# A mixture-of-experts loop made flat: first weights copied by ScalarE, second weights fetched by SyncE, remainders of up to 40 rows in slots

## The chip, the cores and the metric

The kernel runs on one core of a Trainium2 chip. The metric is the device time of one execution in microseconds (us); a kernel's time is the median of its runs. TensorE is called PE in the profile (PEld is its loading of weights), VectorE is DVE, ScalarE is ACT, GpSimd is POOL, and SyncE, which here only issues transfers, is SP.

## What is computed

The input x has 4 sequences of 512 tokens of 128 numbers, 2048 tokens in all. A windowed and latent attention with gates is followed by a residual sum and a layer norm; then comes a mixture of experts, again with residual sum and layer norm. Only the second part is touched by the change, apart from where a few instructions stand:

```python
h = jnp.mod(x_flat[:, :TOP_K].sum(axis=1).astype(jnp.int32), E)
sel = jnp.stack([h, jnp.mod(h + 1, E)], axis=1)
def step(acc, params):
    e, W1e, b1e, W2e, b2e = params
    w = jnp.any(sel == e, axis=1).astype(x.dtype) / TOP_K
    y = jnp.maximum(x_flat @ W1e + b1e, 0.0) @ W2e + b2e
    return (acc + w[:, None] * y, None)
```

W1 is 8 x 128 x 512, W2 is 8 x 512 x 128, all float32. So each token belongs to one of eight groups by a hash of its normed values, and is computed by expert h and expert h + 1 (modulo 8).

## The kernel before

The attention runs over T = 16 tiles of P = 128 tokens, in a software pipeline of T + 3 steps, written out by hand as one instruction list for each engine. Its last step is L1338 with t = T + 2. As tiles are normed, their hash is taken and GpSimd scatters their rows to a memory area seg, in which every group has a segment of its own (L507 to L515). A row there is 129 numbers: the token and its index.

A group is then worked off in tiles of 128 rows. Every tile needs the two halves of the work, for expert e and for e + 1: columns (turn the rows, L1294), up (four matmuls with W1, L1305, into PSUM banks), relu, down (four matmuls with W2, L1323, L1452 and L1459, which add up in bank bY over both experts).

- **Full tiles.** FULL = 5 tiles are known to be full before the last four tiles of attention are through. VectorE finds their experts and rows (full_rows, L933), SyncE fetches both W1 for each into a ring of three buffers w1f (L348 to L353) and the rows into xrow (L362), and TensorE works them off from L1416. TensorE's first columns and first up pass stand inside the attention's last step (L1349, L1351, L1362), with matmuls on spare data among them (keep_busy, L1279). rank_last (L1283) computes the ranks of the last four tiles' tokens, from which VectorE makes their places (place, L894) and the tables (count_tiles, L956), and GpSimd scatters them.
- **The loop.** The remaining tiles come in a loop for each expert (L1441 to L1460), with trip counts from tile_table. All W1 and W2 lie in w1_s and w2_s since the attention. The last tile of a group is filled up by rows that precede the group's, whose index lets nothing be stored. SyncE's loop (L380 to L388) waits until the turn ahead is done (xT_up) and fetches xs, which TensorE turns next, and xrow, which VectorE needs for the residual and GpSimd for the indices. ScalarE does the relus of the first expert and half of the second's (L739, L740), VectorE the other half, the copy of the turned columns (L1051), the residual sum and the moments (L1025 to L1037) and, one tile late, the final norm (finish, L1043), and GpSimd the root (L559) and the store by index (L567).

TensorE's trip, in its order:

```python
up(lambda c: bA, k, w1_s[:, e, :], up_a)
up(lambda c: bB if c < BA else bC, k, w1_s[:, a, :], up_b)
pe.wait_ge(biased, k)
...
columns(k + 1)
...
last.then_inc(down, 1)
```

What is left out is the down half of the first expert (four matmuls of ha with w2_s) ahead of columns, and that of the second (hb) behind it. E is 8 and TOP_K is 2.

Of the kernel before, what the change touches and what calls it, by code (L numbers as in the profile page):

```python
# [13 lines left out]
P = 128  # L14
# [4 lines left out]
def bass_windowed_latent_attention_hash_moe(  # L19
# [23 lines left out]
    BA = FC // 2  # L43
# [5 lines left out]
    SLOTS = T + E + 1  # L49

    with ExitStack() as ctx:
# [84 lines left out]
        tile_table = sb("tile_table", [1, 2, E + 1], I32)  # L136
        full = sb("full", [P, 3, Z + E + 1])
        taken = sb("taken", [P, E])
        jrow = sb("jrow", [P, 2, FULL])
        jint = sb("jint", [P, 2, FULL], I32)  # L140
        reached = sb("reached", [P, FULL, E])
        cover = sb("cover", [P, FULL, E])
        gone = sb("gone", [P, FULL])
        chosen = sb("chosen", [P, FULL, E])
        b1d = sb("b1d", [P, 2, FC, E])
        b1p = sb("b1p", [P, FULL, 2 * FC, E])
        b1x = sb("b1x", [P, FULL, 2 * FC])
        full_table = sb("full_table", [1, 2, FULL], I32)
        tile_scale = sb("tile_scale", [P, E])
        found = sb("found", [P, 2, FULL])  # L150


        w1_s = sb("w1_s", [P, E, F])
        w2_s = sb("w2_s", [P, E, FC, D])
        b1r = sb("b1r", [E * FC, P])
        b1c = sb("b1c", [P, E * FC])
# [3 lines left out]
        fsum = sb("fsum", [P, HEAD, D])  # L160
        w1f = sb("w1f", [P, WR, 2, F])
        xs = sb("xs", [P, D])
        xsT = sb("xsT", [P, P])
        ha = sb("ha", [P, FC, P])
        hb = sb("hb", [P, FC, P])
        ysum = sb("ysum", [P, D])
# [5 lines left out]
        idx = sb("idx", [P, 1], U32)  # L172

# [11 lines left out]
        bA, bB, bX, bY, bC = bS[0][:, 0:512], bS[0][:, 512:1024], bS[1][:, 0:512], bV, bT  # L185

# [49 lines left out]
        b1d_ok = sem("b1d_ok")  # L236
        b1x_ok = sem("b1x_ok")
# [69 lines left out]

        def expand(eng, dst, src, mask, n):

            return eng.tensor_tensor(  # L310
                dst, src.unsqueeze(1).to_broadcast([src.shape[0], n, src.shape[1]]),
                mask.unsqueeze(2).to_broadcast([src.shape[0], n, src.shape[1]]), ALU.mult)

        @block.sync
        def _(sp):
# [12 lines left out]
            load_x(1)  # L328
            sp.dma_start(b1r[:], b1.rearrange("e (c p) -> (e c) p", p=P)).then_inc(b_in, 16)
# [5 lines left out]
            for t in range(T):  # L335
# [6 lines left out]
                if t >= T - E - 4:  # L342
                    e = t - (T - E - 4)
                    if e < E:
                        sp.dma_start(w1_s[:, e, :], W1[e]).then_inc(f_in, 16)
                        sp.dma_start(w2_s[:, e, :, :], W2[e].rearrange("(c p) d -> p c d", p=P)).then_inc(f_in, 16)
# [9 lines left out]
            for j in range(FULL):  # L356
                rows += load_table(sp, full_table[:, 1, :], [j], full_ok, E * SEG - P)
                if j == 0:
                    experts += load_table(sp, full_table[:, 0, :], [j], full_ok, E - 1)
                    load_full_weights(j)  # L360
                    sp.wait_ge(scattered, 16 * EARLY)
                sp.dma_start(xrow[:, j * XW:(j + 1) * XW], seg[bass.ds(rows[j], P), :]).then_inc(full_in[j], 16)  # L362
                if 1 <= j + 1 < WR:
                    experts += load_table(sp, full_table[:, 0, :], [j + 1], full_ok, E - 1)
                    load_full_weights(j + 1)
            for j in range(WR, FULL):
                experts += load_table(sp, full_table[:, 0, :], [j], full_ok, E - 1)
                load_full_weights(j)

            tail = load_table(sp, tail_table, [0], tails_ok, E * SEG - P)  # L370
            first = [FULL] + load_table(sp, tile_table[:, 0, :], [1], table_ok, T + E, FULL)
# [4 lines left out]
            for e in range(E):  # L376
                if e > 0:
                    tail += load_table(sp, tail_table, [e], tails_ok, E * SEG - P)
                    first += load_table(sp, tile_table[:, 0, :], [e + 1], table_ok, T + E, FULL)
                with sp.Fori(first[e], first[e + 1]) as k:  # L380
                    i = nc.s_assert_within(k - first[e], 0, T - 1,
                                           skip_runtime_bounds_check_because="a group has at most all T tiles")
                    row = nc.s_assert_within(tail[e] - i * P, 0, E * SEG - P,
                                             skip_runtime_bounds_check_because="rows of no token precede a group's")
# [5 lines left out]
            sp.wait_ge(xT_up, first[E])  # L390
# [3 lines left out]
        def _(pool):  # L394
# [52 lines left out]
            def routing_constants():  # L447
# [11 lines left out]
                link(nc.gpsimd.tensor_scalar(tile_scale[:], efl[:, 0:E], -1.0 / P, 0.5 / P - 0.5, ALU.mult, ALU.add))  # L459
                link(nc.gpsimd.iota(x1[:, :, D].bitcast(I32), pattern=[[P, T]], base=0, channel_multiplier=1))  # L460
                link(nc.gpsimd.iota(jint[:, 0, :], pattern=[[1, FULL]], base=0, channel_multiplier=0))
                link(nc.gpsimd.iota(jint[:, 1, :], pattern=[[P, FULL]], base=P, channel_multiplier=0))
                nc.gpsimd.tensor_copy(jrow[:], jint[:]).then_inc(jrow_ok, 1)

# [1023 lines left out]
```

## Time and profile before

| | us |
|---|---|
| median of 3 runs | 238.8 (237.17 to 240.47) |
| the profiled execution's own time | 238.23 |
| its span, from the first to the last instruction | 236.5 |
| TensorE busy | 212.2 (90% of the span) |
| VectorE, ScalarE, GpSimd busy | 147.3, 120.6, 117.8 |
| mean granted TensorE clock | 0.986 of full |

The profile is of one execution. Times in its rows count from the span's start. A matmul of float32 is recorded as two records. A row of the chain of work that ended last gives the start, the share of time that the chain spends there, and what; rows of the timeline give start, duration, engine, line and operation. "SPq" and the like are an engine's queue, which issues transfers and does register work.

### The profile page before, as it was taken

How to read it: one execution, taken by the hardware profiler on the slowest of the kernel's cores; microseconds unless marked ns; L12 is line 12 of the kernel's file. 1: busy time of each engine (PE TensorE's matmuls, PEld its weight loads, DVE VectorE, ACT ScalarE, POOL GpSimd, SP SyncE). 2: the span in 40 equal slices, each digit the busy share in tenths (PEclk: the TensorE clock that was granted, in tenths of full speed). 3: DMA queues.
4: the chain of work that ended last, by engine and by line, in shares of the span. 5: the costliest groups of instructions: out<-in, count | busy, mean ns of one | idle time of the engine just before them, and what ended most of it. 6: DMA issues, size and time to landing. Idle time of an engine off the chain costs nothing.

```text
span 236.5 us, 10737 instructions
## 1 busy us (share of the span) xinstructions
PE 212.2 (90%) x4009; PEld 176.2 (75%) x4009; DVE 147.3 (62%) x521; ACT 120.6 (51%) x360; POOL 117.8 (50%) x219
## 2 busy tenths in 40 slices
PE   6879999999998999998999988999999999999920
PEld 2445778767777667886776678989999999899920
DVE  6836448585877765888898616734655555555540
ACT  3546557765466646765656145754344434344400
POOL 6563034852544427762647601847646545455541
PEclk9999999999999999999999999999999999999995
DMA  4131120112232132130001365212121212121100
GB/s 100 58 94 47 49 96 3 45 52 91 91 78 66 47 103 72 43 96 15 28 25 36 117 201 151 96 38 76 40 62 44 56 43 57 27 48 36 35 22 7
DMA packets 18557, 14.73 MB, mean 62 GB/s; under 512 B 2647, under 2 KB 15547, under 8 KB 18513
## 3 DMA queue, kind: packets, MB, share of 16 engines
q1 hardware_dynamic: 17008, 11.83, 17.9%
q0 software_dynamic: 1216, 2.16, 2.8%
q8 instruction: 30, 0.49, 0.9%
q10 hardware_dynamic: 288, 0.13, 0.3%
q14 instruction: 15, 0.11, 0.2%
HBM read 11.43 MB, written 3.03 MB: 61 GB/s over the span
## 4 chain that ended last, share of the span: by engine, by line
PE 74%; DVE 6%; issue 5%; DMA 4%; POOL 3%; ACT 3%; SPq 1%; POOLq 0%; ACTq 0%; DVEq 0%
PE bS L1308 12%; PE bT L1251 7%; PE bV L1452 6%; PE bV L1459 5%; PE bS L1194 4%; PE bV L1266 4%; PE bS L1219 4%; PE bJ L1170 3%; PE bV L1323 3%; PE bT L1308 3%; PE bS L1233 2%; PE bL L1367 2%; PE bS L1201 2%; PE bV L1274 2%; DMA out<-yo,idx 2%
## 5 line engine op out<-in xcount | busy, mean ns | idle before, releaser
L680 ACT ACTIVATE ha<-bS,b1c 128x128 f32<-128x128 f32 x68 | 19.4, 368 | 38.0 <-PE bS L1308 38.0
L668 ACT COPY PTs<-bT 128x512 f32<-128x512 f32 (+3 forms) x48 | 25.9, 539 | 18.2 <-PE bT L1251 18.2
L567 POOL DMA_INDIRECT out<-yo,idx x18 | 19.4, 1076 | 17.5 <-POOL idx L563 9.6
L1251 PE MATMUL bT<-ident,Pr 128*128 128x128 f32 x168 | 27.2, 277 | 0.5 <-issue 0.4
L1308 PE MATMUL bS<-xsT,w_s 128*128 128x128 f32 x204 | 26.3, 279 | 1.1 <-issue 1.0
L1308 PEld LDWEIGHTS bS<-xsT,w_s 128*128 128x128 f32 x204 | 24.1, 192 | 2.2 <-issue 2.2
L498 POOL TENSOR_SCALAR rstd<-mv 128x1 f32<-128x1 f32 x16 | 3.8, 236 | 44.0 <-DVE mv L859 44.0
L1251 PEld LDWEIGHTS bT<-ident,Pr 128*128 128x128 f32 x168 | 19.5, 141 | 5.4 <-issue 4.1
L514 POOL DMA_INDIRECT groups<-x,pos x16 | 16.5, 1034 | 11.7 <-DVE pos L909 8.4
L655 ACT ACTIVATE Pr<-bS 128x512 f32<-128x512 f32 x32 | 20.1, 629 | 3.0 <-PE bS L1233 3.0
L814 DVE TENSOR_REDUCE mx<-bS 128x8 bf16<-128x512 f32 x32 | 21.4, 677 | 0.0
L819 DVE TENSOR_REDUCE mx<-bS 128x8 bf16<-128x128 f32 (+3 forms) x16 | 7.9, 491 | 20.6 <-issue 14.9
L1459 PE MATMUL bV<-w_s,hb 128*128 128x128 f32 x136 | 18.5, 277 | 0.0
L1452 PE MATMUL bV<-w_s,ha 128*128 128x128 f32 x136 | 18.1, 276 | 0.2 <-DVE ysum L1027 0.2
L1077 DVE TENSOR_SCALAR hb<-bT,b1c 128x128 f32<-128x128 f32 x34 | 10.5, 347 | 11.7 <-PE bT L1308 11.0
L1459 PEld LDWEIGHTS bV<-w_s,hb 128*128 128x128 f32 x136 | 16.7, 191 | 0.3
L1452 PEld LDWEIGHTS bV<-w_s,ha 128*128 128x128 f32 x136 | 16.5, 192 | 0.4 <-ACT ha L680 0.4
L1266 PE MATMUL bV<-Vx,PTs 128*32 128x18 f32 x1024 | 15.2, 186 | 1.3 <-DVE rem L835 0.8
L1266 PEld LDWEIGHTS bV<-Vx,PTs 128*32 128x32 f32 x1024 | 12.4, 111 | 4.5 <-issue 3.2
L631 ACT COPY Vx<-bJ 64x256 f32<-64x256 f32 x32 | 12.0, 374 | 7.0 <-PE bJ L1170 6.8
L504 POOL TENSOR_SCALAR x<-y,mv,rstd 128x128 f32<-128x128 f32 x15 | 13.0, 867 | 1.6
L559 POOL TENSOR_TENSOR rstd<-rstd,half 128x1 f32<-128x1 f32 x22 | 12.5, 567 | 1.7
(237 smaller groups left out, 496.9 us busy)
## 6 DMA issues: line engine op xcount, KB each, us to landing
w_s<-in_L_ffn_W SPq DMA_DIRECT2D x16, 256.0 KB
w1f<-in_L_ffn_W SPq DMA_DIRECT2D x10, 256.0 KB, 3.0
xrow<-groups SPq DMA_DIRECT2D x22, 64.5 KB, 1.9
xs<-groups SPq DMA_DIRECT2D x18, 64.0 KB
x_tok<-in_L_attn_x SPq DMA_DIRECT2D x4, 256.0 KB, 3.7
groups<-padrows SPq DMA_DIRECT2D x1, 516.0 KB, 6.0
b2r<-in_L_ffn_b SPq DMA_DIRECT2D x1, 512.0 KB, 3.4
out<-yo,idx POOLq DMA_INDIRECT x18
```

Source lines behind the costliest of these rows:

```text
L504: nc.gpsimd.tensor_scalar(x1[:, t, 0:D], y[:, q, :], mv[:, q, 0:1], rstd[:, q, :], ALU.subtract, ALU.mult).then_inc(ln_done, 1)
L514: nc.gpsimd.indirect_dma_start(seg, bass.IndirectOffsetOnAxis(ap=pos[:, t:t + 1], axis=0), x1[:, t, :], None).then_inc(done, 16)
L567: nc.gpsimd.indirect_dma_start(rows_out, bass.IndirectOffsetOnAxis(ap=idx[:], axis=0), yo[:, FULL - 1, :], None, bounds_check=T * P - 1, o ...
L655: nc.scalar.activation(Pr[:, t % 2, j, :].rearrange("p (z c) -> p z c", z=2), own[j], ACT.Exp, scale=SCALE).then_inc(exped[j], 1)
L668: nc.scalar.copy(PTs[:, j, 0:m, :], bT[:, 0:m * P].rearrange("p (c q) -> p c q", c=m)).then_inc(turned_out, 1)
L680: nc.scalar.activation(dst[:, c, :], src[:, c * P:(c + 1) * P], ACT.Relu, bias=bias_of(c)).then_inc(relu, 1)
L814: nc.vector.tensor_reduce(mx[:, j, :].rearrange("p (z h) -> p z h", z=2), own[j].rearrange("p z (h k) -> p z h k", h=4), AX.X, ALU.max).th ...
L1251: last = nc.tensor.transpose(bT[:, c * P:(c + 1) * P], Pr[:, t % 2, j, c * P:(c + 1) * P], ident[:])
L1266: last = mm(bV[i * W:(i + 1) * W, a * PW:(a + 1) * PW], PTs[:, j, c, i * W:(i + 1) * W], Vx[:, q, i, a, :], start=True, stop=True)
L1308: last = mm(bank_of(c)[:, c * P:(c + 1) * P], w[:, c * P:(c + 1) * P], xsT[:], start=True, stop=True)
L1452: mm(bY[:, 0:D], ha[:, c, :], w2_s[:, e, c, :], start=(c == 0), stop=False)
L1459: last = mm(bY[:, 0:D], hb[:, c, :], w2_s[:, a, c, :], start=False, stop=(c == FC - 1))
```

## The change

- **Slots.** A group's last rows, up to TS = 40, no longer make a tile. The last 40 rows of each of the eight groups are fetched into xt (three tiles of 3, 3 and 2 groups), turned ahead of the loop, and after the loop each expert does one pass over the 80 columns of its two groups (slot_pass_up, slot_pass_down), with outputs that are transposed and turned back, and residual, norm and store of their own.
- **One flat loop.** All other tiles behind the five full ones run in one loop with one trip count, by a table with an entry for each tile: row, expert, next expert. VectorE makes it in count_tiles, with more operations.
- **First weights.** In the loop TensorE reads w1a and w1b, single buffers. ScalarE copies the next tile's there out of w1_s, behind its relus.
- **Second weights.** TensorE reads w2a and w2b, single buffers as well. SyncE fetches them from memory for each tile: w2a when the first down half is done (half_down), w2b when the second is (down). The fetch of the next tile's rows stands between the two.
- **The front.** The first up passes of the full tiles stand behind the attention's last step, not in it, and most of the keep_busy matmuls around them are gone. The biases are read from b1c by a register, not gathered ahead into b1x.

Core of the diff (SyncE, ScalarE, TensorE, then the slots):

```diff
-                with sp.Fori(first[e], first[e + 1]) as k:
...
-                    sp.wait_ge(kept, k * 16)
-                    sp.wait_ge(xT_up, k)
-                    sp.dma_start(xs[:], seg[bass.ds(row, P), 0:D]).then_inc(tile_in, 16)
-                    sp.dma_start(xrow[:, bass.ds(k * XW, XW)], seg[bass.ds(row, P), :]).then_inc(kept, 16)
+            def load_tile(k, row):
+                sp.wait_ge(kept, k * 16)
+                sp.wait_ge(xT_up, k)
+                sp.dma_start(xs[:], seg[bass.ds(row, P), 0:D]).then_inc(tile_in, 16)
+                sp.dma_start(xrow[:, bass.ds(k * XW, XW)], seg[bass.ds(row, P), :]).then_inc(kept, 16)
+            tail = load_table(sp, tail_table, range(E), tails_ok, E * SEG - TS)
+            last = load_bound(sp)
...
+            for s, w1_to in ((0, w1a), (1, w1b)):
+                sp.dma_start(w1_to[:].unsqueeze(1),
+                             W1[bass.ds((e + s) % E, 1)].rearrange("e p f -> p e f")).then_inc(first_in, 16)
+            load_w2(w2a, e, w2a_ok)
+            load_w2(w2b, (e + 1) % E, w2b_ok)
...
+            load_tile(FULL, row)
+            for g in range(E):
+                h = (g % GT) * TS
+                sp.dma_start(xt[h:h + TS, g // GT, :], seg[bass.ds(tail[g], TS), :]).then_inc(tail_in[g // GT], 16)
+            with sp.Fori(FULL, last1) as k:
+                at = entry_of(k) + 1
...
+                sp.wait_ge(half_down, k + 1)
+                load_w2(w2a, e, w2a_ok)
+                load_tile(k + 1, row)
+                sp.wait_ge(down, k + 1)
+                load_w2(w2b, (e + 1) % E, w2b_ok)

+            with act.Fori(FULL, last) as k:
...
+                for c in range(FC):
+                    nc.scalar.activation(ha[:, c, :], bA[:, c * P:(c + 1) * P], ACT.Relu,
+                                         bias=bias_of(e)(c)).then_inc(relu, 1)
+                after = load_next(act, k)
...
+                nc.scalar.copy(w1a[:], w1v[:, bass.ds(after * F, F)]).then_inc(w1a_ok, 1)
+                act.wait_ge(up_b, k + 1)
...
+                nc.scalar.copy(w1b[:], w1v[:, bass.ds(after * F + F, F)]).then_inc(w1b_ok, 1)

+            pe.wait_ge(tail_out, 2)
+            with pe.Fori(FULL, last) as k:
+                pe.wait_ge(w1a_ok, k + 1)
+                up(lambda c: bA, k, w1a, up_a)
+                pe.wait_ge(w1b_ok, k + 1)
+                up(lambda c: bB if c < BA else bC, k, w1b, up_b)
+                pe.wait_ge(y_ok, k)
+                pe.wait_ge(w2a_ok, k * 16 + 16)
...
+                    i = mm(bL[:, 0:D], ha[:, c, :], w2a[:, c * P:(c + 1) * P], start=(c == 0), stop=False)
+                i.then_inc(half_down, 1)
+                columns(k + 1)
+                pe.wait_ge(w2b_ok, k * 16 + 16)
...
+                    i = mm(bL[:, 0:D], hb[:, c, :], w2b[:, c * P:(c + 1) * P], start=False, stop=(c == FC - 1))
+                i.then_inc(down, 1)

+            for i in range(E + 2):
+                if i < E:
+                    slot_pass_up(i)
+                if i >= 2:
+                    slot_pass_down(i - 2)
```

SyncE's queue, one trip of its loop before, with the semaphores that a row waits for:

```order
L380 UNCONDITIONAL_BRANCH
L380 ISA
L387 ISA [waits xT_up,kept]
L387 DMA xs<-groups 128x128
L388 ISA
L388 DMA xrow<-groups 128x129
L380 REGISTER_ALU
L380 COMPARE_AND_BRANCH
```

And the same loop now (table is the new table of tiles, groups the memory area seg, w2a and w2b the buffers of the second weights):

```order
L474 TENSOR_LOAD table
L474 ISA x2
L476 REGISTER_ALU
L457 ISA [waits half_down]
L457 DMA w2a<-in_L_ffn_W 128x4x128
L445 REGISTER_ALU
L447 ISA [waits xT_up,kept]
L447 DMA xs<-groups 128x128
L448 ISA
L448 DMA xrow<-groups 128x129
L457 ISA [waits down]
L457 DMA w2b<-in_L_ffn_W 128x4x128
```

The fetch of xs, which stood behind the turn alone, stands behind half_down and a fetch of 256 KB. On TensorE the second half of its trip is now this (bL is the bank of the sum, bS the bank of the turned columns; half_down is given by the last of the w2a matmuls):

```order
L1655 REGISTER_ALU
L1656 MATMUL bL<-w2a,ha 128x128 [waits relu]
L1514 ISA
L1516 MATMUL bS<-ident,xs 128x128 [waits xT_out,tile_in]
L1662 REGISTER_ALU [waits w2b_ok]
L1665 MATMUL bL<-w2b,hb 128x128 [waits relu]
```

The turn of xs stands directly behind the matmul that gives half_down, as it stood behind its counterpart before. At the attention's last step TensorE had this before:

```order
L1299 MATMUL bS<-ident,xrow 128x128 [waits full_in0]
L1281 MATMUL bJ<-spare 128x256 x4
L1308 MATMUL bS<-xsT,w1f 128x128 [waits xT_out,w1f_in0]
L1308 MATMUL bS<-xsT,w1f 128x128 x3
L306 TENSOR_LOAD full_table [waits full_ok,f_in]
L306 ISA x2
L306 TENSOR_LOAD full_table
L306 ISA x2
L1281 MATMUL bJ<-spare 128x256 x2
L1358 MATMUL bL<-ident,att 128x128 [waits gated]
```

And it has this now:

```order
L1562 MATMUL bL<-ident,att 128x128 [waits gated]
L1512 MATMUL bS<-ident,xrow 128x128 [waits full_in0]
L1494 MATMUL bJ<-spare 128x256 x4
L1571 MATMUL bL<-wout_s,attT 128x128 [waits attT_out]
L354 TENSOR_LOAD table [waits full_ok,f_in]
L354 ISA x2
L354 TENSOR_LOAD table
L354 ISA x2
L1521 MATMUL bS<-xsT,w1f 128x128 [waits xT_out,w1f_in0]
```

The turn of the last tile's attention and its projection (wout_s) moved ahead of the first up pass and of the two table loads.

## Rows read from the trace of the kernel before

**Rows 1.** The page: busy time by engine, and shares of the chain that ended last.

```profile
PE 212.2 (90%) x4009; PEld 176.2 (75%) x4009; DVE 147.3 (62%) x521; ACT 120.6 (51%) x360; POOL 117.8 (50%) x219
...
PE 74%; DVE 6%; issue 5%; DMA 4%; POOL 3%; ACT 3%; SPq 1%; POOLq 0%; ACTq 0%; DVEq 0%
```

**Rows 2.** The chain that ended last, one steady tile: start us, us, what.

```profile
183.33 1.34 PE bS L1308 x12
184.67 0.45 PE bT L1308 x4
185.12 0.89 PE bV L1452 x8
186.01 0.11 PE bS L1303
186.12 0.89 PE bV L1459 x8
187.01 1.34 PE bS L1308 x12
```

**Rows 3.** Groups of instructions by line: the two store lines.

```profile
L567 POOL DMA_INDIRECT out<-yo,idx x18 | 19.4, 1076 | 17.5 <-POOL idx L563 9.6 <-DVE yo L1045 7.9
...
L578 POOL DMA_INDIRECT out<-yo,xrow x4 | 4.1, 1017 | 3.9 <-DVE yo L1045 3.4 <-issue 0.5
```

**Rows 4.** The chain again, the loop's start and its one late tile.

```profile
159.69 1.34 PE bS L1308 x12
...
162.37 0.12 PE bS L1303
...
162.79 0.33 SPq L387
...
163.32 1.78 DMA xrow<-groups
...
165.50 1.15 PE bV L1452 x8
...
169.93 0.89 PE bV L1452 x8
```

**Rows 5.** Timeline of the end: start us, us, engine, line, what.

```profile
225.27 1.06 PE L1459 MATMUL bV<-w_s,hb 128*128 128x128 f32 x8
...
230.59 1.05 POOL L567 DMA_INDIRECT out<-yo,idx  x1 [0.85 <-POOL idx L563]
```

**Rows 6.** DMA issues of the page: KB each, us to landing.

```profile
w1f<-in_L_ffn_W SPq DMA_DIRECT2D x10, 256.0 KB, 3.0
```

**Rows 7.** The chain around the attention's last step.

```profile
133.86 2.48 DMA xrow<-groups
...
137.16 1.13 PE bS L1308 x8
...
140.57 0.30 DVE y L855
```

**Rows 8.** A stretch of half a microsecond: busy by engine, PEclk, DMA share, GB/s.

```profile
63.00:63.50 0.50, 0.50 (x18) 0.38 (x5) 0.23 (x1) 0.02 (x1) 0.00 (x0) 1.00 0.31 87
```

**Rows 9.** Timeline: a copy and four relus of ScalarE, matmuls in quarters.

```profile
103.98 0.71 PE L1274 MATMUL bV<-GVx,PTs 128*32 128x72 f32 x32
...
64.08 0.59 ACT L668 COPY PTs<-bT 128x512 f32<-128x512 f32 x1 [1.06 <-PE bT L1251]
...
139.61 1.15 ACT L680 ACTIVATE ha<-bS,b1x 128x128 f32<-128x128 f32 x4
```

**Rows 10.** SyncE's loads of one table: ns min/median/max, first and last start.

```profile
L306 SPq TENSOR_LOAD <-tail_table x8: 264/272/277, 147.2 to 207.3; - x8
```

**Rows 11.** Timeline of VectorE: the last of its table operations.

```profile
149.28 0.26 DVE L970 CAST tile_table<-tiles 1x9 int32<-1x9 f32 x1
```

**Rows 12.** Stretches after the last matmul; PEclk is the third number from the right.

```profile
226.40:230.00 3.60, 0.00 (x0) 0.00 (x0) 1.48 (x5) 0.00 (x0) 2.10 (x4) 1.00 0.05 18
230.00:231.00 1.00, 0.00 (x0) 0.00 (x0) 0.00 (x0) 0.00 (x0) 0.41 (x1) 0.50 0.00 0
```

More of the change, by code:

```diff
@@ L159, in bass_windowed_latent_attention_hash_moe @@
         xrow = sb("xrow", [P, SLOTS * XW])
-        fsum = sb("fsum", [P, HEAD, D])
+        b2q = sb("b2q", [E, D])
+        share = sb("share", [E, E, TS])
+        fsum = sb("fsum", [P, FULL, D])
         w1f = sb("w1f", [P, WR, 2, F])
+        w1a, w1b, w2a, w2b = (sb(n, [P, F]) for n in ("w1a", "w1b", "w2a", "w2b"))
         xs = sb("xs", [P, D])
@@ L701, in _ @@
                 if t == T + 1:
[L702 removed]
+                    for s in (w1a_ok, w1b_ok):
+                        act.sem_inc(s, FULL + 1)
+                    act.sem_inc(half_down, FULL)
+                    experts = load_table(act, experts1, [0, 1], full_ok, E - 1)
                 if 1 <= t <= T:
@@ new lines, in slot_pass_down @@
+            def slot_pass_down(i):
+                e = ORDER[i]
+                hid = slot_hidden[i % 3][0]
+                groups = (0, E - 1) if e == 0 else (e - 1, e)
+                parts = [(groups[0], 0), (groups[1], 1)] if e % GT == 0 else [(groups[0], 0)]
+                for c in range(FC):
+                    pe.wait_ge(slot_relu, FC * i + c + 1)
+                    for g, q in parts:
+                        n = TS if len(parts) == 2 else 2 * TS
+                        at = (g % GT) * TS
+                        for h in range(2):
+                            last_down = mm(slot_sum[g // GT][h * HF:(h + 1) * HF, at:at + n],
+                                           w2_s[:, e, c, h * HF:(h + 1) * HF], hid[:, c, q * TS:q * TS + n],
+                                           start=False, stop=False, skip_group_check=True)
+                last_down.then_inc(slot_down, 1)
@@ new lines, in slot_biases, with turn_back @@
+            def slot_biases(t):
+                gs = groups_of(t)
+                mm(slot_sum[t][:, 0:len(gs) * TS], b2q[:],
+                   share[:, gs.start:gs.stop, :].rearrange("p g r -> p (g r)"), start=True, stop=False,
+                   skip_group_check=True)
+            def turn_back(t):
+                n = len(groups_of(t)) * TS
+                pe.wait_ge(tail_flat, t + 1)
+                if t == 1:
+                    pe.wait_ge(y_ok, last)
+                if t == 2:
+                    pe.wait_ge(tail_y, 1)
+                nc.tensor.transpose(slot_back[t][0:n, 0:D],
+                                    ysT[:, t * GT:t * GT + len(groups_of(t)), :].rearrange("p g r -> p (g r)"),
+                                    ident[:]).then_inc(tail_back, 1)
@@ new lines, in _ @@
+            pe.wait_ge(b2q_in, 16)
+            pe.wait_ge(share_ok, 1)
+            pe.wait_ge(f_out, FULL)
+            pe.wait_ge(tail_out, TT)
+            for t in range(TT):
+                slot_biases(t)
+            pe.wait_ge(xT_out, last + 1)
+            back = 0
+            for i in range(E + 2):
[3 more added lines that the diff above has]
+                    slot_pass_down(i - 2)
+                while back < TT and i - 3 >= max(ORDER.index((g + s) % E) for g in groups_of(back) for s in range(2)):
+                    turn_back(back)
+                    back += 1
```

540 lines of the change are left out of this document (350 added, 190 removed).

## Prediction

> **What bounds the kernel now.** I read the page first, then the chain that ended last from 130 us to the end, then single stretches of it. TensorE is busy 90% of the span and carries 74% of the chain; no other engine has more than 6% [rows 1]. In the expert loop a tile costs 3.68 us: twelve records of the first up passes, four of the last, eight of the first down half, the turn of the next tile's columns, eight of the second down half, with no gap [rows 2]. The loop has 17 trips, since one store line has 18 stores (the fifth full tile is one of them) and the other 4, so 22 tiles in all [rows 3]. It starts at 159.69 [rows 4] and its last matmul ends at 226.3 [rows 5]: 66.6 us, 3.9 us a tile. At a change of expert some tenths are lost, and one tile, whose rows came late, stands out. There SyncE wakes after the turn of the columns, issues xs 0.30 us later and xrow 0.53 us after that, which lands 1.78 us on; only then do VectorE and TensorE go on. From this delayed down half to the next tile's (165.50 to 169.93) it is 4.43 us instead of 3.68: after a stop the next groups run slower [rows 4]. The span ends 10.2 us after the last matmul, on GpSimd's stores [rows 5].
>
> **How many tiles the changed loop has.** The reference's inputs give the eight groups 1052, 324, 132, 35, 10, 29, 131 and 335 tokens. Rounded up to 128 that is 22 tiles, as in the trace. The changed kernel leaves up to 40 rows of each group to a slot: 8+3+1+0+0+0+1+3 = 16 tiles, 5 of them full ones ahead of the loop, so 11 trips, and eight slot passes behind them.
>
> **The wait that the change adds.** SyncE now waits in each trip for half_down, the first down half of tile k, then issues the 256 KB of w2a, and only behind it xs and xrow of tile k+1. TensorE's next instruction after that same down half is the turn of tile k+1, which waits for xs. Before, xs was asked for as soon as the turn ahead of it was done, a whole tile early. Nothing can hide the fetch any more: behind the waiting turn are queued the second down half and all of the next tile, and VectorE's copy of xsT, its residual and GpSimd's store wait for these. Price: 0.30 us to the first issue; some 0.6 to xs (two plain issues lie 0.53 apart [rows 4], and here are a register operation and two waits more); 1.8 to landing, as xrow has. That is 2.7 us. It also queues behind w2a. A w1f of 256 KB needs 3.0 from issue to landing [rows 6], and an xrow behind two of them landed 2.48 after its issue [rows 7]; so 0.3 + 3.0 = 3.3 as upper end. W2's rows are shorter, but a W1 and a W2 that were issued together from 60.3 to 61.1 moved until about 63.2, as the DMA share falls off there [rows 8]. I take 2.9, between 0.9 + 1.8 and 0.9 + 2.48. To it comes the slower running after a stop: 0.26 us (1.15 for 0.89, one group) to 0.75 (all of them) [rows 4]; I take 0.5. So 3.4 us for each of ten trips (the eleventh's turn reads rows fetched early): 34 us, bounds 29 and 43.
>
> The Trainium skill ("DMA: Bandwidth & Descriptors", Queues, rings and completion order) says that a completion signal is a strongly ordered write, which lands only after every earlier write of that DMA engine; so the signal of xs could not come before w2a's data. By it the wait is the 3.3 us and not 2.9, and the ten are 38 us; the 2.48 us row bears it out halfway, since the transfers ahead of that one had a head start.
>
> **The other parts, step by step.**
> - Six tiles fewer: 6 x 3.9 = 23.5 us gone. The remaining 11 run in one loop without changes of expert, so 3.68 and not 3.92 each: 2.6 us more gone. From 66.6 to 40.5.
> - ScalarE's copies of w1a and w1b (128x512 each; such a copy out of PSUM takes 0.59) and a table load of some 0.5: with six relus at 0.29 (1.15 for four) that is 3.4 us a trip [rows 9]. Beside a 7 us trip it costs nothing. If the fetch wait were gone it would be level with TensorE. In the first trip ScalarE comes late, having three copies and two loads to do: 0.8.
> - w2b is issued after the last down and is needed 2.7 us plus the fetch wait later: hidden. The same for w2a itself, and for the bias and residual rows of VectorE, which now fall into the wait.
> - The front. The turn and the projection of the last tile no longer stand behind the first up pass and the two table loads, which took from 137.16 to the 140.57 at which VectorE's chain to the ranks starts [rows 7]. That now starts at about 137.4 and, 4.5 us long, is done at 141.9, ahead of where rank_last stands (142.7), so TensorE's 0.9 us stop there goes. The full tiles start at 138.0 and take 5 x 3.68 plus 1.0 for ranks and loads: done at 157.4 instead of 159.7.
> - But the loop can't start then. SyncE has eight table loads where it had one, each about 0.5 us (0.27 and its register work [rows 10]); from tail_table at 145.4 (ranks 142.7, placing 2.2, a load 0.5) to 149.4. VectorE's tables take 23 small operations where they took 12, at some 0.2: ready near 150.0 (149.5 before [rows 11]). Then two loads, four weight transfers at 0.6, two loads, xs at 154.6 (landed 156.6, about when TensorE asks for it), xrow, and eight transfers of 40 rows at 0.5: the last lands at 161.0. TensorE turns these rows ahead of the loop. Loop start 161.5, so 1.8 later than before; bounds 160 and 164.
> - The slots. Eight up and eight down passes of eight matmuls of 80 columns on half the array's width. One after another they take 80/128 of the 0.89 us that eight records of 128 columns take, but twice over: 1.1 us each, 18 in all. In four quarters side by side 32 records of 72 columns took 0.71 [rows 9]; in halves I put 0.7 a pass, 11.2, and 0.8 for filling and emptying: 12 us. ScalarE's 32 relus at 0.29 are 9.1, the lower end.
> - The end. From the last slot down: flatten, turn back, residual, two moments, two steps of the deviation, finish and one store ahead, at 0.2 to 1.05 each with a handover: about 4.5 us to the start of the last store, from which the span had 5.9 left (230.59 to 236.5 [rows 5]): 10.4, as good as now (10.2).
>
> **Sum.** 161.5 + (3.7 + 3.4 + 0.8) + 9 x 7.1 + 3.7 = 237.0 for the loop's end; + 12 = 249.0; + 10.4 = 259.4 as span; + 1.7 that the profiled execution has outside its span (238.23 against 236.5) = 261 us. That execution lies at the median of 238.8, so the forecast is for the median too: slower by 9%.
>
> **Rivals.**
> - *Not slower: the fetch of xs is hidden after all.* If the signals let SyncE run one tile ahead, the loop is 11 x 3.75 = 41 us and the time 261 - 35 = 226. For it: ScalarE presets half_down for the full tiles, and xs has its own buffer. Against: the preset is five, so the first trip waits for its own tile's half, and no transfer of this trace lands in under 1.8 us. It ends level with now when the extra per tile is under 1.3 us. Faster 0.02, level 0.04.
> - *The clock falls.* TensorE would stand still 2.9 us in each 7. Each trip's 3.7 us would double and the slots too: 261 + 40 = 300 at the worst, 280 if it falls in half of the trips. Against: after the last matmul the granted clock stayed full for 3.6 us and fell to half only then [rows 12]; here matmuls come back after 2.9. 0.07.
>   The Trainium skill ("TensorE: Matmul & The Clock Gate", HAM oscillation) tells of just such a loop, matmuls and then a DMA wait per tile, that fell back to 1.2 GHz in every tile; by it the time is the 300 and not 261.
> - *The fetch costs more,* because the 512 short rows of w2a hold xs up beyond 4 us: with 4.5 for 2.9 the time is 277. For it: 128 rows of 2 KB took 3.0 us, 512 rows have never been waited for here. 0.12.
>
> **Chances.** Forecast as worked out 0.75. Range 248 to 275: the low end has the wait at 2.7 and 0.25 after it, slots at 9 and the start at 160, and 3 us more; the high end the wait at its upper bound and half of the slots', or the third rival. A change under 2% is about what can't be told from none. Faster 0.02, same 0.05, slower 0.93.
>
> **What would show it.** Right: a steady trip of 6.6 to 7.6 us; TensorE's idle time ahead of the turn of xs, released by the DMA of xs, near 2.9 us ten times; ScalarE idle on TensorE in the loop; loop start 160 to 164; slots of 10 to 14 us. Wrong: trips of 3.7 to 4 us, or a granted clock under 0.9 in the loop, or waits at w2a or w1a in place of xs, or a number of trips other than 11.

## The result, and the profile after

The changed kernel takes 290.4 us (median of 4 runs, 288.9 to 292.1) against 238.6 (237.2 to 240.5): a ratio of 1.214, 95% interval 1.208 to 1.221. The forecast was 261, with a range up to 275. The direction was right and the size was not: 52 us were lost where 22 were expected. Some executions in experiments 3 (one of four) and 9 (three of ten) were in a slower state; the ratios leave them out, and the fast ones have medians of 286.3 and 244.0 us.

The page of the changed kernel: its engines, the rows of PE and of the granted clock in 40 slices, the chain by engine, and of the groups the turn of xs and ScalarE's relus (busy, mean ns | idle before, releaser). They answer to [rows 1].

```profile
span 287.6 us, 11092 instructions
PE 226.0 (79%) x4113; PEld 189.3 (66%) x4113; DVE 140.5 (49%) x498; ACT 131.9 (46%) x383; POOL 112.2 (39%) x208
...
PE   7788999999989979988799567555577558759940
...
PEclk9999999999999999999799867977777676577995
...
PE 67%; DMA 10%; issue 7%; SPq 7%; DVE 4%; ACT 2%; POOL 1%; DVEq 0%; ACTq 0%; POOLq 0%
...
L882 ACT ACTIVATE ha<-bS,b1c 128x128 f32<-128x128 f32 x44 | 12.5, 368 | 67.6 <-PE bS L1521 67.6
...
L1516 PE MATMUL bS<-ident,xs 128*128 128x128 f32 x12 | 4.8, 398 | 35.3 <-DMA xs<-groups 35.3
```

Two things are to be seen. TensorE waits 35.3 us for the DMA of xs: that is the wait that the change adds. And from the 23rd to the 37th slice, which is the loop, the clock is at 0.5 to 0.9 of full; over the whole span its mean is 0.886, where the kernel before had 0.986. TensorE was busy for 226 us instead of 212. It has six tiles of 33 records fewer (22 us, 6 x 3.68 [rows 2]) and the slots' 313 smaller records more (11.6 us), so at full clock it would have been busy for less time than before, not more.

The windows of the changed kernel's loop, one row for each trip, cut at the turns of xs; the column behind POOL's is the granted clock. The last row is the slots.

```profile
164.40:173.40 9.00, 5.49 (x25) 5.20 (x24) 1.90 (x7) 3.20 (x10) 1.93 (x4) 0.65 0.21 61
173.40:182.40 9.00, 5.55 (x33) 5.36 (x33) 2.22 (x8) 2.79 (x8) 1.98 (x4) 0.81 0.28 82
182.40:189.80 7.40, 3.98 (x33) 3.79 (x33) 2.19 (x8) 2.79 (x8) 2.00 (x4) 1.00 0.33 97
189.80:198.80 9.00, 5.59 (x33) 5.41 (x33) 2.19 (x8) 2.84 (x8) 2.00 (x4) 0.76 0.28 81
198.80:208.80 10.00, 6.70 (x33) 6.51 (x33) 2.19 (x8) 2.83 (x8) 1.98 (x4) 0.67 0.25 72
...
256.70:264.50 7.80, 7.76 (x43) 7.64 (x43) 3.00 (x11) 2.84 (x8) 1.98 (x4) 0.61 0.17 51
264.50:276.10 11.60, 11.60 (x313) 11.05 (x312) 2.77 (x10) 7.40 (x32) 3.90 (x7) 1.00 0.05 15
```

All trips between two turns that waited have the same 33 records of PE; the first row begins with the loop, and the row from 256.70 goes on to the loop's end, with no wait in it. One of them ran at full clock throughout and took 7.40 us, 3.98 of it busy; the others took 8.6 to 10.2, with 5.2 to 6.7 busy. Idle time is 3.3 to 3.5 us in each of them, whatever the clock. So a trip has two costs, one that is always there (the wait) and one that comes and goes (the clock).

The chain of the changed kernel (start, time on the chain, what) in the trip at full clock, and below the last mark the beginning of one at half clock:

```profile
182.44 0.33 PE bS L1516
182.77 0.91 PE bL L1665 x8
183.68 1.37 PE bS L1521 x12
185.05 0.45 PE bT L1521 x4
185.50 0.94 PE bL L1656 x8
...
186.72 0.39 SPq L457
...
187.45 2.33 DMA xs<-groups
...
189.82 0.33 PE bS L1516
...
198.83 0.47 PE bS L1516
199.30 1.71 PE bL L1665 x8
201.01 2.56 PE bS L1521 x12
```

The first down half ends at 186.44 and the turn starts at 189.82: 3.4 us. SyncE issues w2a (L457) 0.28 after the half and xs 0.73 after w2a, and xs lands 2.33 after that. On the critical path nothing but this chain and TensorE's own groups is left. ScalarE idles on TensorE 67.6 us: it bounds nothing. At half clock the same eight records take 1.71 for 0.91.

Where the time of the profiled execution (289.4) goes beside the forecast (261.1): start of the loop 164.6 for 161.5 (+3.1), the 11 trips 99.9 for 75.5 (+24.4), slots 11.5 for 12 (-0.5), end 11.6 for 10.4 (+1.2), outside the span 1.8 for 1.7 (+0.1).

### The profile page after: what moved, and what is told of

Its sections match the earlier page's. It is cut to its first block, busy times and chain, and to the rows that moved or that the text cites. A ratio compares the mean times of both kernels' runs of the same rounds, so it can differ in the third digit from the quotient of the medians.

```text
span 287.6 us, 11092 instructions
## 1 busy us (share of the span) xinstructions
PE 226.0 (79%) x4113; PEld 189.3 (66%) x4113; DVE 140.5 (49%) x498; ACT 131.9 (46%) x383; POOL 112.2 (39%) x208
## 4 chain that ended last, share of the span: by engine, by line
PE 67%; DMA 10%; issue 7%; SPq 7%; DVE 4%; ACT 2%; POOL 1%; DVEq 0%; ACTq 0%; POOLq 0%
PE bS L1521 11%; DMA xs<-groups 8%; PE bT L1464 6%; PE bL L1665 5%; PE bL L1656 4%; PE bS L1407 3%; PE bV L1479 3%; PE bS L1432 3%; PE bJ L1383 3%; PE bT L1521 3%; SPq L354 2%; PE bS L1446 2%; PE bL L1571 2%; SPq L457 2%; PE bV L1487 2%
## 5 line engine op out<-in xcount | busy, mean ns | idle before, releaser
L882 ACT ACTIVATE ha<-bS,b1c 128x128 f32<-128x128 f32 x44 | 12.5, 368 | 67.6 <-PE bS L1521 67.6
L669 POOL DMA_INDIRECT out<-yo,idx x12 | 12.6, 1050 | 58.6 <-DVE yo L1214 57.7
L1516 PE MATMUL bS<-ident,xs 128*128 128x128 f32 x12 | 4.8, 398 | 35.3 <-DMA xs<-groups 35.3
L1220 DVE COPY xsT<-bS 128x128 f32<-128x128 f32 x11 | 3.2, 292 | 41.0 <-PE bS L1516 41.0
L1521 PE MATMUL bS<-xsT,w1a 128*128 128x128 f32 x88 | 19.8, 401 | 0.2 <-issue 0.2
L1521 PEld LDWEIGHTS bS<-xsT,w1a 128*128 128x128 f32 x88 | 18.5, 310 | 0.3 <-issue 0.3
L1249 DVE TENSOR_SCALAR hb<-bT,b1c 128x128 f32<-128x128 f32 x22 | 6.7, 346 | 24.3 <-PE bT L1521 24.3
L1665 PE MATMUL bL<-w2b,hb 128*128 128x128 f32 x88 | 17.4, 365 | 0.0
L1665 PEld LDWEIGHTS bL<-w2b,hb 128*128 128x128 f32 x88 | 16.1, 274 | 0.0
L983 DVE TENSOR_REDUCE mx<-bS 128x8 bf16<-128x128 f32 (+3 forms) x16 | 7.9, 491 | 16.7 <-issue 12.4
L1383 PE MATMUL bJ<-wvg,xT 128*32 128x64 f32 (+1 forms) x512 | 12.4, 228 | 2.9 <-issue 2.6
```

The costliest lines, as they stand in the source:

```text
L669: nc.gpsimd.indirect_dma_start(rows_out, bass.IndirectOffsetOnAxis(ap=idx[:], axis=0), yo[:, FULL - 1, :], None, bounds_check=T * P - 1, o ...
L882: nc.scalar.activation(ha[:, c, :], bA[:, c * P:(c + 1) * P], ACT.Relu, bias=bias_of(e)(c)).then_inc(relu, 1)
L1383: last = mm(bJ[r * W:(r + 1) * W, at:at + wide], xT[:, b % 2, w:w + W], wvg[:, c, 0:wide], start=True, stop=True)
L1521: last = mm(bank_of(c)[:, c * P:(c + 1) * P], w[:, c * P:(c + 1) * P], xsT[:], start=True, stop=True)
L1665: i = mm(bL[:, 0:D], hb[:, c, :], w2b[:, c * P:(c + 1) * P], start=False, stop=(c == FC - 1))
```

## The experiments

Runs of one group shared the runs of the kernel before, 238.6 to 240.3 us, and each ratio is to those. "Trip" is the time from one turn of xs to the next. "After" is the changed kernel; each edit is to it unless said otherwise.

**1. Is the rest the clock?** Spare matmuls fill the wait; nothing comes earlier.

```diff
                 i.then_inc(half_down, 1)
+                keep_busy(26)
                 columns(k + 1)
```

> 26 matmuls on spare data (256 columns, bf16) fill TensorE's wait between the first down half and the turn of xs; the wait itself stays. Theory C (fetch wait 3.4 us in ten trips, and on top of it the granted clock that the waits bring down): the clock is back at full, every trip takes 7.3 to 7.6 as the one full-clock trip of the changed kernel did, the 11 trips 79 to 82 us instead of 99.9, the kernel 268 to 273. Theory F (the transfers alone: the longer trips come from later landings, and TensorE's slower records only stretch over a wait that is there anyway): trips stay at 9 to 10, the kernel 286 to 292.

271.5 us (270.0 to 272.8), ratio 1.135 [1.126, 1.144]: 18.9 us less than after, though TensorE has more to do. The window of one steady trip of this kernel:

```profile
189.30:196.70 7.40, 6.97 (x63) 6.41 (x62) 2.33 (x9) 2.79 (x8) 2.00 (x4) 1.00 0.34 98
```

The clock is full, and the nine steady trips take 7.26 to 7.50 us (6.6 to 7.6 had been forecast for after). So 18.9 us of the loss are the clock, and that is a lower bound: in the last trip, which has no wait, the fill is pure extra work (6.63 us from turn to turn, where the kernel of experiment 5 without W2 fetches took 3.84), and the first trip's up passes still run at half clock (0.50 from 165.0 to 168.8), as in after; ahead of the loop TensorE has waits that nothing fills. DMA, SyncE and ScalarE do the same work in the same time as in after, and xs lands 2.1 to 2.4 us after its issue in all ten trips of after that wait for it, long or short, which rules out that TensorE's long trips there come from a slower transfer.

**2. A shorter fill.** keep_busy(8) in place of 26, some 0.9 us of work.

> The kernel after with 8 spare matmuls (about 0.9 us) between the first down half and the turn of xs, where the warm kernel had 26 (3.0 us). No wait of the program is shortened: xs comes 3.4 us after the half, so 2.5 us of idleness stay in each trip instead of 3.4. Theory 1 (the clock falls on how long TensorE stands still in each trip, and 2.4 us was enough for one trip in three in the kernel without W2 fetches, 2.2 us for half of the trips in the kernel before with the wait): the clock falls in some trips and not in most, 273 to 282 us, between the warm kernel's 271.5 and after's 290.4. Rival (any wait of over 2 us costs the clock in most trips at this tile length): 286 to 291. Rival (the clock falls only after an idleness of 3 us or more in one piece): 270 to 273, with a granted clock of 0.96.

276.3 us (273.5 to 276.9), 1.144 [1.135, 1.153], granted clock 0.933. Behind the first trip five take 7.3 to 7.5 us and four 8.8 to 8.9. The page's row of the clock in 40 slices, with the loop in the right half:

```profile
PEclk9999999999999997999979986789997998999985
```

With 2.5 us idle in a trip (26.5 us at the turns in all) instead of 3.4 the clock falls in four of nine steady trips (0.81 to 0.83 in each, 1.00 in the other five) and costs 1.5 us when it does. The times alone wouldn't tell this kernel from that of experiment 1, since their intervals overlap and the short fill saves 2 us in the last trip; the trips do. The first theory holds in this loop, and both rivals' times are missed: the loss grows with the standstill. The fill also adds matmuls, so these runs don't tell less idle time from more work.

**3. The wait by itself, in the kernel before.** Its xs waits for the first down half as well, whose last matmul now raises half_down; everything else is the old kernel's.

```diff
                     sp.wait_ge(xT_up, k)
+                    sp.wait_ge(half_down, k)
                     sp.dma_start(xs[:], seg[bass.ds(row, P), 0:D]).then_inc(tile_in, 16)
```

> The kernel before, with one wait added: SyncE fetches xs of a tile only when the first down half of the tile ahead is done. All else as before: 17 trips, weights in SBUF. The wait is then 0.3 for SyncE and 2.0 for xs, 2.3 to 2.6 in each of 16 trips. If the clock stays full: 238.6 + 16 x 2.5 = 276 to 282. If it falls in one of three trips, as with the wait of 2.5 us without W2 fetches, 8 us more: 284 to 292. If it falls in every trip: over 300.

287.6 us (285.0 to 289.3), ratio 1.202 [1.192, 1.212]. One semaphore wait costs the kernel before nearly as much (49 us) as the whole change does (52). The parts are not the same, though: here it is 16 waits of 2.2 us and seven slow trips, there ten waits of 3.4 and a slower clock in most trips, less six tiles. The turns of this kernel:

```profile
L1306 PE MATMUL bS<-ident,xs 128*128 128x128 f32 x18 | 6.4, 356 | 35.7 <-DMA xs<-groups 35.7
```

The chain of this kernel around one wait, and then the windows behind this wait and behind the next:

```profile
186.64 0.91 PE bV L1455 x8
...
187.88 1.83 DMA xs<-groups
...
189.76 0.47 PE bS L1306
```

```profile
190.50:193.00 2.50, 2.50 (x14) 2.50 (x14) 1.09 (x5) 0.00 (x0) 1.05 (x1) 0.52 0.00 0
...
197.20:199.00 1.80, 1.67 (x15) 1.67 (x16) 0.83 (x3) 0.00 (x0) 0.00 (x0) 1.00 0.10 28
```

Here TensorE stands still only 2.1 to 2.4 us, since no w2a is ahead of xs (1.83 to landing for 2.33). Of 17 trips seven take 7.6 to 7.9 us at a clock of 0.78 or 0.79, nine 6.05 to 6.8 at 0.98 to 1.00, and the last, with no wait, 3.76: the clock falls in fewer than half. This trace is of the slowest of the four runs (289.3), so seven may be on the high side. Behind the wait that ended at 189.76 it was at half for three microseconds of matmuls, behind the next, of the same length, it stayed full. Of the three times expected this is the middle one, in which the clock falls in some trips.

**4. What the w2a ahead of xs costs.** The two fetches of W2 in SyncE's loop are left out, their semaphores are raised in the same places, so TensorE reads the first tile's second weights in every trip.

```diff
                 sp.wait_ge(half_down, k + 1)
-                load_w2(w2a, e, w2a_ok)
+                sp.sem_inc(w2a_ok, 16)
                 load_tile(k + 1, row)
                 sp.wait_ge(down, k + 1)
-                load_w2(w2b, (e + 1) % E, w2b_ok)
+                sp.sem_inc(w2b_ok, 16)
```

> Leaves out the fetches of second weights in the loop (all tiles use those of the loop's first tile); SyncE's order is kept, xs still behind half_down. Shows what w2a's issue and transfer have in the wait for xs. If xs merely starts later by w2a's issue (0.45 to 0.7), the wait falls from 3.4 to about 2.7; if it also queues behind the data, to 2.3 to 2.5. Clock: idle stretches of 2.5 in 6.3. If it stays full, trips 6.2 to 6.5 and the kernel 290.4 - 99.9 + 68 = 258 to 261; if it still falls, 268 to 280.

264.5 us (264.2 to 265.2), 1.107 [1.100, 1.115]. The turns of this kernel wait 25.6 us for xs where after's wait 35.3:

```profile
L1516 PE MATMUL bS<-ident,xs 128*128 128x128 f32 x12 | 4.5, 374 | 25.6 <-DMA xs<-groups 25.6
```

So w2a's issue and transfer are 1.0 us of the 3.4, and 2.4 come from the order of the waits alone. The trips take 6.3 to 6.4 us, and every third one 7.7 to 8.0, at a clock of 0.78 or 0.79: at 2.4 us of standstill the clock falls in a third of the trips. The fetches cost 26 us in after, about 10 of them as wait and most of the rest through the clock (three slow steady trips here, eight there).

**5. The order without its wait.** The rows of tile k+1 are fetched ahead of the wait for half_down:

```diff
+                load_tile(k + 1, row)
                 sp.wait_ge(half_down, k + 1)
                 load_w2(w2a, e, w2a_ok)
-                load_tile(k + 1, row)
                 sp.wait_ge(down, k + 1)
                 load_w2(w2b, (e + 1) % E, w2b_ok)
```

> SyncE fetches xs and xrow of tile k+1 ahead of its wait for half_down, as soon as the turn of tile k is done; w2a and w2b as in the changed kernel. Theory C: the wait at the turn of xs goes; w2a, issued 0.3 after the half and 2.9 to 3.1 in landing, is needed 2.8 after it, so a wait of 0.4 to 0.7 appears there; clock full; trips 4.1 to 4.5, loop 46 to 50 us, kernel 236 to 241. Rival W (w2a is the true limit, the turn of xs only shows it first): w2a's wait takes over, trips over 6 us, kernel over 258.

251.9 us (250.6 to 253.8), 1.053 [1.045, 1.061]. 38 us of the 52 come back by moving one line; the 236 to 241 were missed. The trips take 5.8 to 6.6 us, and the turns still wait 16.7. The clock fell in two of the nine steady trips (0.72 and 0.74), behind waits of 1.8 and 1.9 us; one of these trips, 6.02 us, was hardly longer for it, because the rows it would have waited for came only then. Each trip of SyncE begins only when down of the tile ahead has come, with w2b, a branch and two table loads in a row: from the end of down at 182.3 to the issue of xs at 185.0 in one trip, and 2.06 to landing. The theory was too simple: xs had lost one wait and not the queue ahead of it. With no W2 fetched in this order either (both edits):

> Leaves out the same fetches and has xs early too: no fetch wait of any kind. What is left is ScalarE's chain (six relus, two copies, one table load: 3.4 us of work) against TensorE's 3.68. If that chain is hidden, trips 3.7 to 3.9, loop 41 to 43, kernel 231 to 234; if it is the next limit (its copy of w1a needs the relus and a table load after the first up pass), trips 4.1 to 4.6 and the kernel 236 to 241.

247.1 us (246.7 to 248.3), 1.034 [1.027, 1.042], steady trips of 5.25 us, 12.8 us of waiting left at the turns: a branch and two table loads (2.2 us from the end of down to the issue of xs) stand behind down(k), so the rows are late even with no weights in the queue. A miss too, for the same reason.

**6. Rows fetched two tiles ahead.** Table entry and rows of tile k+2 behind w2a.

```diff
                 sp.wait_ge(half_down, k + 1)
                 load_w2(w2a, e, w2a_ok)
-                load_tile(k + 1, row)
+                load_tile(k + 2, row)
                 sp.wait_ge(down, k + 1)
                 load_w2(w2b, (e + 1) % E, w2b_ok)
```

> SyncE fetches the rows of tile k+2 where the changed kernel fetches those of k+1 (behind w2a of tile k+1); the loads of W2 stay as they are. The rows have a whole trip, so no wait at the turn of xs. If the earlier version with the rows moved only ahead of half_down was held by SyncE's own sequence (down, w2b, two table loads, xs: 5.9 us trips), that is gone here. Theory C: w2a, needed 2.8 us after the half and landing 3.0 to 3.4 after it, is the only wait, 0.3 to 0.8; trips 4.1 to 4.6, clock full, kernel 236 to 241. Rival (256 KB fetches twice a tile are the limit by themselves): trips 5.5 and more, kernel over 250.

242.6 us (242.0 to 244.3), 1.018 [1.011, 1.025], 1.6 above the range that had been expected. No turn in the loop waits for xs any more, and from the fourth trip on they take 4.4 to 4.7 us. The chain of this kernel shows what is late next:

```profile
187.85 0.94 PE bL L1656 x8
...
188.96 0.39 SPq L457
...
190.83 3.13 DMA w2b<-in_L_ffn_W
...
194.07 1.15 PE bL L1665 x8
```

It is w2b, issued at 190.8 behind w2a, xs and xrow, 3.13 to landing: TensorE's second down half waits for it in six of eleven trips (0.4 to 1.2 us). In three others it waits 0.3 to 0.5 us for ScalarE's relus of hb, so a second limit lies close behind.

**7. No second weights fetched at all.** As 6, but TensorE reads them in w2_s, where they lie since the attention (w2f is a flat view of it), by a register that it loads from the table once a trip.

```diff
-                pe.wait_ge(w2a_ok, k * 16 + 16)
+                e = pe.snap(kept_expert, min_val=0, max_val=E - 1)
...
-                    i = mm(bL[:, 0:D], ha[:, c, :], w2a[:, c * P:(c + 1) * P], start=(c == 0), stop=False)
+                    i = mm(bL[:, 0:D], ha[:, c, :], w2f[:, bass.ds(e * F + c * P, P)], start=(c == 0), stop=False)
```

> Rows two tiles ahead, and TensorE reads the second weights out of w2_s at an address from a register; no fetch of them in the loop. Left are ScalarE's copies of first weights. Theory C: TensorE's 3.68 us is the trip, 3.7 to 4.0 with a table load on TensorE; loop 42 to 45 us, kernel 232 to 236. Rival (ScalarE's chain of four relus, table load, copy, two relus, copy limits): trips 4.2 to 4.6, kernel 238 to 242.

252.2 us (251.0 to 254.5), 1.060 [1.051, 1.068], a clear miss: trips of 5.5 us with no transfer in them. The chain of this kernel:

```profile
181.38 0.89 issue
182.26 1.14 PE bS L1516 x8
...
183.99 0.28 ACTq L372
...
185.22 0.36 ACT hb L886
...
185.71 1.19 PE bL L1660 x8
```

TensorE's own sequencer now stands 0.9 us at the register load ahead of the up pass, and then the relus, ScalarE's table load and its copy of w1a stand between the up pass and the relus of hb. These 3.45 us from 182.26 to the down half, with 1.2 and 0.9 behind them, are a ring in which nothing overlaps (5.54 us, the trip). The fetches of W2 were thus not the only thing that the flat loop has to hide.

**8. The front.** Spare matmuls (8, 6 and 6) in the attention's last step of after.

> The changed kernel with spare matmuls put back into the attention's last step, ahead of its turn (6), of columns(0) (8) and of the table loads (6); the loop is untouched. Theory C: the clock is full at the first two up passes, which take 1.8 us in place of 3.65; the ranks and with them the tables and the loop's start come 1.9 us earlier (162.7 for 164.6); kernel 288 to 289. Rival (loop start is set by SyncE's table loads alone): start unchanged at 164 to 165, kernel as the changed one, 290.4.

290.9 us (289.3 to 291.7), 1.218 [1.210, 1.226]: no change. The first two up passes took 2.02 us instead of 3.65, but began at 141.5 instead of 139.8, and the loop started at 164.69 as against 164.58. This tells little of the spare matmuls, since the kernel of experiment 5 shows the same with no edit there: its first passes began at 140.8 and took 2.02. In the profiles of the seven kernels whose front is the same (after and the edits of experiments 1, 2, 4, 5 and 6), these passes begin at 138.4 to 141.1 (3.6 to 3.75 us long in the four that begin before 140, 2.0 to 2.75 in the other three), and the loop starts at 164.2 to 165.0. So an early beginning gains nothing at the loop's start; why it goes with a low clock stays open.

**9. A version that beats both?** On top of 6: the tails' turn and copy behind the loop, their table loads between the rows of the first two tiles, their fetches behind SyncE's loop.

> The two-tiles-ahead kernel (242.6 us) with the slots' work taken from in front of the loop: the turn and copy of the tail rows stand behind the loop, their eight fetches behind SyncE's loop, and their eight table loads between the rows of the first and of the second loop tile. Theory: the loop's start hangs on the xs of the first tile (landed at about 160) and no longer on the last tail row (164.0), so the loop starts at 160.6 to 161.5 instead of 164.6, and its first two trips, which took 10.0 us in the kernel two tiles ahead, get shorter; the tail rows' fetches take 8 x 0.53 and 2 us to land from the moment the last but one tile is down, a tile and a half before the slots, so up to 2 us come back there. 237 to 241 us. Rival (SyncE's table loads only move the wait to the second weights of the second trip): 241 to 244.

244.9 us (241.6 to 247.0, 10 runs), 1.015 [1.010, 1.020], level with 6 within the intervals. The first trip fell from 10.0 to 5.9 us, but in the profiled execution, the slowest of the ten, its turn came at 164.0 instead of 160.1 (161.0 in the next kernel), and the slots began with a wait for the last of the tail rows, which were issued 214.6 to 218.0 and landed at 219.8. Theory and rival each had a part. With w2b ahead of the rows in SyncE's loop on top of that:

```diff
                 load_w2(w2a, e, w2a_ok)
-                load_tile(k + 2, row)
                 sp.wait_ge(down, k + 1)
                 load_w2(w2b, (e + 1) % E, w2b_ok)
+                load_tile(k + 2, row)
```

> As the kernel with late tails, and in SyncE's loop the fetch of w2b stands ahead of the fetch of the rows instead of behind it. Theory: in the kernel two tiles ahead TensorE waits in each trip for w2b, which lands 3.2 to 3.4 us after its issue, behind xs and xrow, and is issued only after these; with w2b issued at once after down it lands in about 3.0 and is there 0.5 us or more earlier, while the rows have a tile's time in hand. Trips of 4.0 to 4.3 us instead of 4.55: 3 to 5 us less than the kernel with late tails, 233 to 238, so faster than both kernels. Rival (ScalarE's chain of relus, copies and a table load bounds the trip at about 4.5 whatever lands): within 1 us of the kernel with late tails.

247.7 us (246.8 to 249.8), 1.031 [1.023, 1.039]: both theory and rival missed. The turns wait again, 0.4 to 0.8 us in most trips: xs lands 2.3 to 3.2 us after its issue (186.2 for an issue at 183.2, say), now behind 256 KB of w2b, and trips take 4.5 to 5.4. With the spare matmuls of experiment 8 as well:

> As the kernel with w2b first, and with the spare matmuls in the attention's last step of which the run on the front told. Theory: the loop's start hangs now on the full tiles' end and the first xs, and no longer on the tails; the first two up passes at full clock take 2.0 for 3.65 us, so the full tiles end up to 1.6 us earlier, of which the first xs (landed at about 160) lets through little: 0 to 1 us less than the kernel with w2b first. Rival (the spare matmuls hold up the attention's last step, as the aT at 138.4 for 136.9 in the run on the front hinted): 0 to 1.5 us more.

246.3 us (245.8 to 247.1), 1.023 [1.016, 1.029], 1.4 less than without the spare matmuls; the intervals overlap, so that gain is not shown. No version beat the kernel before; the best two, 6 and the first of 9, come to within 1.8 and 1.5% of it.

## Why the prediction was wrong

- **The step that failed** is the argument against the second rival: "after the last matmul the granted clock stayed full for 3.6 us and fell to half only then; here matmuls come back after 2.9". One wait behind 230 us of dense work was taken as the price list for waits that recur in every trip. The runs show the clock falling inside or just behind waits of 3.4 us (after), and of 2.1 to 2.5 us (experiments 2 to 4), in part of the trips. What the sum put at nothing cost 18.9 us and more. That rival had been given 0.07, and the measured 290.4 lies between its two times, 300 if the clock falls in every trip and 280 if in half: in after it fell in ten of eleven trips, in part of each. That these times fit so well is in part luck. The 40 us to the 300 are eleven times 3.7 and leave out the slots, which the same sentence has doubling too (12 more); as it came out the slots ran at full clock. The Trainium skill ("TensorE: Matmul & The Clock Gate", HAM oscillation) describes such a loop, with the clock back at 1.2 GHz in every tile. The rows of after agree in kind but not in full: one steady trip of nine kept 1.00, and the others lost it for part of their length. The row that seemed to speak against it was a different case. One sign that had been named for being wrong, a granted clock under 0.9 in the loop, was met in ten of eleven trips.
- **The wait,** forecast at 2.9, is 3.4. Its parts: 0.28 to w2a's issue (0.30), 0.73 more to xs (0.6), 2.33 to landing (2.0). xs lands 3.06 after w2a's issue, which is what a fetch of 256 KB needs by itself (3.0 [rows 6]). The Trainium skill ("DMA: Bandwidth & Descriptors", Queues, rings and completion order) had given 3.3 by its rule on signals, and that was the better number; no run here tells this rule from a plain queueing of xs behind w2a's data. Ten times 0.5 are 5 us, of which 2 come back by the slower running after a stop: 0.3 (3.98 busy for 3.68), not 0.5. At full clock a trip is 7.4, for 7.1.
- **The eleven trips,** forecast at 75.5, are 99.9 in after. From turn to turn the nine steady trips take 83.3 us, where nine at full clock take 66.4 (7.38 each): 16.9 for the clock. The last takes 6.6 at a clock of 0.61, for 3.7: 2.9 more. The waits' share is 2.5 (nine times 7.38 for 7.1). From the loop's start to the first turn that waited it is 8.9 us for 6.9 (7.9 less the 1.0 of a turn and a second down half): 2.0, with the clock at 0.50 over the first up passes (164.4 to 168.0), behind waits of 1.3, 0.8 and 0.4 us for rows ahead of the loop. That is 24.3 of the 24.4. Experiment 1 gives back 17.5 of them from the first to the last turn (102.7 and 85.2), or 18.9 by the medians, for the two reasons named there.
- **Loop start,** 161.5 forecast, bounds 160 and 164, is 164.6, just outside. The full tiles were to start at 138.0. In the changed kernel's chain (SPq L354 is one half of a table load; the fetches of the tail rows are L471) their first two up passes begin 1.8 later and run at half clock, 3.65 us where 1.8 had been reckoned:

```profile
138.95 0.84 issue
139.79 3.65 PE bS L1521 x16
...
148.40 0.43 DVE tail_table L1120
148.84 0.27 SPq L354
...
158.06 0.35 SPq L447
...
162.44 1.55 DMA xt<-groups
...
164.58 0.55 PE bS L1521
```

  TensorE so comes to rank_last 3.6 us late, and the eight loads of tail_table start at 148.84, forecast 145.4. From there it went nearly as reckoned: xs goes out 9.2 us later (9.2 forecast), the last tail row lands at 163.99 (161.0).
- **Right:** 11 trips; the wait at xs, released by its DMA, on the path and in all ten trips that have it; ScalarE hidden; the slots, 11.5 for 12; w2b hidden behind the wait. The end is 11.6 for 10.4; the last of the three slot stores starts 5.6 us ahead of the span's end (5.9 forecast), so the 1.2 lie between the last down and that store.
- **The first rival** (the fetch hidden) was rightly given almost nothing. **The third** (fetch at 4.5) didn't occur: 3.4. Its 277 us lie outside the range up to 275 that was said to hold it, and the upper bound of 43 us for ten waits is more than its own parts give (0.9 + 2.48 + 0.75, so 41); neither touches the forecast.
- **The cause** is thus shown from both ends: the wait alone makes the kernel before nearly as slow as the changed one (experiment 3), moving it away gives 38 of 52 us (5) and 48 (6), and filling it gives 19 without shortening it (1).

## What to carry to other kernels

A new wait in a TensorE loop is priced twice: for its length, and for the clock that it takes from the work around it, here 34 us for ten waits and some 20 more. A granted clock that survives one stop says nothing of a loop with a stop in every trip; if the trace before has no such loop, the range must hold the case that it falls. And a serial queue is to be read as a chain: moving a transfer ahead of one wait gained only what lay between that wait and the next thing ahead of it (experiments 5 to 7).

## What the runs showed of the hardware

The same standstill gave different clocks. In after, these windows lie around two neighbouring waits, the first without a fall in it, the second with one:

```profile
187.40:188.40 1.00, 0.00 (x0) 0.00 (x0) 0.00 (x0) 0.14 (x1) 0.00 (x0) 1.00 0.28 84
188.40:189.80 1.40, 0.00 (x0) 0.00 (x0) 0.00 (x0) 0.00 (x0) 0.00 (x0) 1.00 0.78 219
189.80:190.80 1.00, 0.98 (x9) 0.98 (x9) 0.61 (x3) 0.00 (x0) 0.00 (x0) 1.00 0.01 4
190.80:192.50 1.70, 1.70 (x11) 1.70 (x10) 0.94 (x4) 0.00 (x0) 0.86 (x1) 0.59 0.02 7
192.50:194.40 1.90, 1.90 (x11) 1.90 (x10) 0.03 (x1) 1.53 (x5) 0.96 (x3) 0.50 0.55 166
...
196.50:197.50 1.00, 0.00 (x0) 0.00 (x0) 0.00 (x0) 0.00 (x0) 0.00 (x0) 1.00 0.55 167
197.50:198.50 1.00, 0.00 (x0) 0.00 (x0) 0.00 (x0) 0.00 (x0) 0.00 (x0) 0.71 0.80 208
198.50:199.50 1.00, 0.67 (x3) 0.67 (x4) 0.16 (x1) 0.00 (x0) 0.00 (x0) 0.50 0.07 19
```

The wait of 3.4 us that ended at 189.8 passed at full clock, 2.4 GHz, and the clock fell to half, 1.2 GHz, between one and one and a half microseconds after TensorE was busy again; it was back at full by 194.8, ahead of the next wait. In that wait it fell while TensorE stood still, and came back only after the matmuls of nearly a whole trip (0.50 up to 204.5 by the same view). So the trip that pays may be the one after the one that waited, and a trip loses 1.2 to 2.8 us (8.6 to 10.2 against 7.4), according to how much of it falls into the low stretch.
